# Delta rule: ScalarE's affine step on the turned output stays in its PSUM bank, VectorE's gate product reads it there, and the steps of all four engines are put in another order

## What is computed

```
q, k, v = silu(causal_conv4(x @ Wq)), silu(causal_conv4(x @ Wk)), silu(causal_conv4(x @ Wv))
alpha, beta = sigmoid(x @ Wa + ba), sigmoid(x @ Wb + bb)
for each token t:
    err = S k_t - v_t
    S = alpha_t S - beta_t err k_t^T
    o_t = S q_t
o = layernorm(o) * ln_w + ln_b            # over the 128 values of a head
o = o * sigmoid(x @ Wg)                   # the gate
y = o @ Wo
```

## Time and profile before

| what | value |
|---|---|
| runs | median 1885.67 us of 3 (1882.06 to 1886.81) |
| profiled execution | 1887.38 us, its span 1885.6 us, TensorE's mean granted clock 0.977 |
| busy in the span | PE 1781.6, PEld 1315.9, DVE 1529.9, ACT 1286.9, POOL 941.3 us |
| four laps, 812.0 to 949.4 us | 137.40 us: PE busy 135.95, DVE 125.06, ACT 105.42, POOL 86.21 us, clock 1.00 |
| the gate product (L1910), 64 times | 675 / 1152 / 2193 ns (least, median, most) |
| the affine step (L1804), 64 times | 768 / 772 / 777 ns |

### The profile page before, as it was taken

The page is one execution under the profiler, slowest core; times in us unless marked ns, Lnnn a source line. Parts: engine busy times, 40 slices in busy tenths (PEclk is TensorE's granted clock), DMA queues, the critical chain, the costliest instruction groups (busy, mean ns, idle before and its releaser), DMA issues.

```text
span 1885.6 us, 49242 instructions
## 1 busy us (share of the span) xinstructions
PE 1781.6 (94%) x19366; PEld 1315.9 (70%) x19366; DVE 1529.9 (81%) x2561; ACT 1286.9 (68%) x2850; POOL 941.3 (50%) x1890
## 2 busy tenths in 40 slices
PE   8889999999899889999999999999999999999687
PEld 4733333332688767888888888888888888887576
DVE  6699999993466567989989999899899898998455
ACT  2068888889342357778777777787777777777553
POOL 1134344445223244666566566666666566565233
PEclk9989999999899999999999999999999999999889
DMA  6201212110100111111111111111111111110101
GB/s 184 85 17 35 59 35 59 34 47 8 29 1 1 56 35 36 49 38 35 49 49 35 39 50 38 35 50 49 35 50 38 35 50 38 35 38 20 45 1 45
DMA packets 74133, 78.61 MB, mean 42 GB/s; under 512 B 13168, under 2 KB 60784, under 8 KB 73904
## 3 DMA queue, kind: packets, MB, share of 16 engines
q1 hardware_dynamic: 73904, 75.46, 13.6%
HBM read 66.13 MB, written 8.91 MB: 40 GB/s over the span
## 4 chain that ended last, share of the span: by engine, by line
PE 38%; ACT 14%; DVE 9%; issue 4%; POOL 1%; POOLq 0%; ACTq 0%; DVEq 0%
PE ps L1530 10%; PE ps L1678 5%; PE ps L1560 4%; DVE d_acc L1833 3%; PE ps L1660 3%; ACT d_kq L1717 3%; ACT d_tt L1769 2%; PE ps L1648 2%; PE ps L1654 2%; PE ps L1630 2%; ACT d_acc L1701 2%; PE ps L1637 2%; DVE d_o_g L1910 2%; PE ps L2008 1%; ACT d_ty L1766 1%
## 5 line engine op out<-in xcount | busy, mean ns | idle before, releaser
L1833 DVE SCALAR_TENSOR_TENSOR d_acc<-ps,d_par,d_acc 128x1023 f32<-128x1023 f32 (+2 forms) x288 | 366.1, 1271 | 25.7 <-ACT d_acc L1701 25.5
L601 ACT ACTIVATE a_prob<-ps 128x512 f32<-128x512 f32 (+2 forms) x640 | 309.3, 563 | 99.1 <-PE ps L567 93.9
L1530 PE MATMUL ps<-x1p,d_wh 128*128 128x512 f32 x1024 | 358.7, 431 | 7.1 <-DVE d_acc L1833 7.1
L623 DVE TENSOR_REDUCE a_mx<-ps 128x2 f32<-128x1024 f32 (+2 forms) x320 | 336.5, 1112 | 34.9 <-PE ps L551 27.2
L1530 PE MATMUL ps<-x1p,d_wl 128*128 128x512 f32 x512 | 203.1, 397 | 0.0
L510 POOL TENSOR_SCALAR_AFFINE_SELECT a_prob<-a_prob 128x128 f32<-128x128 f32 (+1 forms) x384 | 125.2, 330 | 125.1 <-ACT a_prob L601 114.1
L567 PE MATMUL ps<-q,k 51*128 51x512 bf16 (+2 forms) x640 | 175.1, 365 | 2.5 <-ACT a_prob L601 0.9
L1701 ACT ACTIVATE d_acc<-ps,d_par 128x512 f32<-128x512 f32 x192 | 145.8, 776 | 42.5 <-PE ps L1530 40.4
L1530 PEld LDWEIGHTS ps<-x1p,d_wh 128*128 128x128 f32 x1024 | 161.1, 191 | 18.4 <-DVE d_acc L1833 8.1
L1785 ACT ACTIVATE d_w_sb<-ps 128x128 f32<-128x128 f32 x256 | 70.5, 275 | 144.9 <-PE ps L1648 144.2
L581 PE MATMUL ps<-a_prob,a_v 128*32 128x512 f32 (+3 forms) x1536 | 165.0, 502 | 0.4 <-POOL a_prob L510 0.2
(11 more groups left out here) (244 smaller groups left out, 4557.4 us busy)
## 6 DMA issues: line engine op xcount, KB each, us to landing
d_abc<-scratch_alpha SPq DMA_DIRECT2D x32, 512.0 KB, 3.9
d_gb<-scratch_g SPq DMA_DIRECT2D x32, 512.0 KB, 4.0
d_wr<-in_dw SPq DMA_DIRECT2D x16, 512.0 KB, 3.5
scratch_q<-p_parts SPq DMA_DIRECT2D x24, 128.0 KB, 2.4
q<-scratch_q SPq DMA_DIRECT2D x32, 96.0 KB
scratch_y<-a_oT SPq DMA_DIRECT2D x64, 36.0 KB
x_tok<-in_x SPq DMA_DIRECT2D x4, 512.0 KB, 7.6
q<-scratch_q SPq DMA_DIRECT2D x32, 64.0 KB
```

Source lines behind the costliest of these rows:

```text
L601: inc(nc.scalar.activation(prob[:, y % PB, g:g + heads, off:], ps[:, PLACE["st", n, x], 0:heads * w].rearrange("p (h c) -> p h c", c=w), A ...
L623: inc(nc.vector.tensor_reduce(out, ps[:, bank:bank + 2, 0:heads * w].rearrange("p r (h c) -> p r h c", c=w), AX.X, ALU.max, negate=True), ...
L1530: last = nc.tensor.matmul(ps[:, bank, :], wp[g][:, k, i, :], x(part), start=(k == 0 and j == 0), stop=(k == KE - 1 and j == 2))
L1833: inc(nc.vector.scalar_tensor_tensor(acc[i][:, d:T], taps[:, 0:T - d], par[p][:, 4 * i + j:4 * i + j + 1], acc[i][:, d:T], ALU.mult, ALU.a ...
```

## The change

ScalarE writes the affine step's result back into the PSUM bank that it read, instead of into `o_g` in SBUF. VectorE's gate product reads that bank and writes `o_g`. So `o_g`'s reuse (`og_l` of unit n-2) is now waited for by VectorE and no longer by ScalarE, and the ring frees `o_turn`'s bank with the gate product (`gated`) instead of with the affine step.

```diff
         def o_turn(n, j):                                        # PE
-            bank = ring(n, ("o_turn", j), ("affine", n, j + 1))
+            bank = ring(n, ("o_turn", j), ("gated", n, j + 1))
...
             W("o_turned", n, j + 1)                              # ACT
-            W("og_l", n - 2, j + 1)
-            inc(nc.scalar.activation(o_g[n % 2][:, j * HALF:(j + 1) * HALF], ps[:, BANK[n, "o_turn", j], :], ACT.Identity, bias=ln2[:, 1:2],
+            bank = ps[:, BANK[n, "o_turn", j], :]
+            inc(nc.scalar.activation(bank, bank, ACT.Identity, bias=ln2[:, 1:2],
                                      scale=ln2[:, 0:1]), "affine")
...
             W("affine", n, j + 1)                                # DVE
+            W("og_l", n - 2, j + 1)
             c = slice(j * HALF, (j + 1) * HALF)
-            inc(nc.vector.scalar_tensor_tensor(o_g[n % 2][:, c], gate[n % 2][:, c], 1.0, o_g[n % 2][:, c], ALU.add, ALU.mult), "gated")
+            inc(nc.vector.scalar_tensor_tensor(o_g[n % 2][:, c], gate[n % 2][:, c], 1.0, ps[:, BANK[n, "o_turn", j], :], ALU.add, ALU.mult), "gated")
```

All four lists of `ORDER` are replaced. The new ones, cut to the stretches that matter below:

```diff
 "PE"
+ L.proj.0.0.0 L.proj.0.0.1 O.ks.2 ... S.k_turn.0 O.w.3 O.qs.3 O.s.3 O.pw.3 S.k_turn.1 O.ks.4 O.qs.4 X.o_turn.0 O.w.4 X.o_turn.1 O.s.4 O.pw.4
+ ... O.ks.6 S.z32 O.w.6 O.qs.6 S.v_turn.0 O.s.6 S.y64 O.ks.7 O.pw.6 S.gate.0.0 S.v_turn.1 O.w.7 S.z64 O.qs.7 O.pw.7 S.gate.0.1 L.proj.2.0.0
+ S.y128 L.proj.2.0.1 L.proj.2.1.0 L.proj.2.1.1 S.z128 L.pair.0 L.pair.1 S.w.0 L.pair.2 S.s.0 X.out.0 L.pair.3 S.ks.1 S.pw.0 X.out.1 S.qs.1
+ S.w.1 X.out.2 S.pw.1 S.s.1 X.out.3
 "ACT"
+ ... S.spread O.w.5 X.og.0 S.y32 O.pw.5 X.og.1 L.tap.1.0 O.w.6 L.tap.1.1 S.diag S.y64 S.v_turn.0 O.pw.6 O.w.7 S.v_turn.1 S.z64 L.silu.0 O.pw.7
 "DVE"
+ X.o_turn.0 S.k_turn.1 S.turned O.pw.3 O.s.5 X.o_turn.1 O.ks.6 S.whole ... S.s.1 L.lanes S.pw.0 S.ks.2 X.out.1 X.out.2 X.out.3 ... L.columns S.ks.5
 "POOL"
- S.solve.1 S.solve.2 S.solve.3 S.solve.4 S.qg X.og.0 L.scalars O.wo L.split O.stats X.og.1 L.solve.0
+ S.solve.4 O.wo X.og.0 L.split X.og.1 L.scalars O.stats S.qg L.solve.0 L.solve.1 L.solve.2 L.solve.3
```

More of the change, by code:

```diff
@@ L1244 @@
     "PE": """
[L1245 to L1248, removed]
@@ L1249 @@
-        S.qs.4 S.s.4 S.pw.4 E.proj.1.0.0 S.ks.5 E.proj.1.0.1 S.w.5""",
+        L.proj.0.0.0 L.proj.0.0.1 O.ks.2 L.proj.0.1.0 O.w.2 L.proj.0.1.1 O.qs.2 O.s.2 O.pw.2 O.gate.1.0 O.ks.3 O.gate.1.1 S.k_turn.0 O.w.3 O.qs.3
+        O.s.3 O.pw.3 S.k_turn.1 O.ks.4 O.qs.4 X.o_turn.0 O.w.4 X.o_turn.1 O.s.4 O.pw.4 L.proj.1.0.0 O.ks.5 L.proj.1.0.1 L.proj.1.1.0 O.w.5 O.qs.5
+        S.y32 O.s.5 O.pw.5 L.proj.1.1.1 O.ks.6 S.z32 O.w.6 O.qs.6 S.v_turn.0 O.s.6 S.y64 O.ks.7 O.pw.6 S.gate.0.0 S.v_turn.1 O.w.7 S.z64 O.qs.7 O.pw.7
@@ L1250 @@
+        S.gate.0.1 L.proj.2.0.0 S.y128 L.proj.2.0.1 L.proj.2.1.0 L.proj.2.1.1 S.z128 L.pair.0 L.pair.1 S.w.0 L.pair.2 S.s.0 X.out.0 L.pair.3 S.ks.1
+        S.pw.0 X.out.1 S.qs.1 S.w.1 X.out.2 S.pw.1 S.s.1 X.out.3""",
     "ACT": """
-        O.w.1 S.blocks O.pw.1 O.w.2 L.tap.0.0 S.silu.2 L.tap.0.1 O.pw.2 O.w.3 X.norm.0 O.gate.1 O.pw.3 S.v_turn.0 O.w.4 X.norm.1 O.pw.4 O.w.5
-        X.o_turn.0 L.tap.1.0 O.pw.5 S.spread L.tap.1.1 O.w.6 S.y32 X.o_turn.1 S.v_turn.1 X.og.0 O.pw.6 S.diag O.w.7 S.y64 L.silu.0 S.z64 O.pw.7
@@ L1253 @@
-        L.silu.1 S.y128 L.tap.2.0 L.tap.2.1 S.gate.0 S.z128 S.w.0 S.pw.0 X.og.1""",
+        S.tap.2.0 S.tap.2.1 O.gate.0 O.z128 O.w.0 X.norm.0 O.pw.0 O.w.1 S.blocks O.pw.1 X.norm.1 L.tap.0.0 O.w.2 L.tap.0.1 O.pw.2 O.w.3 O.gate.1
+        O.pw.3 O.w.4 S.silu.2 X.o_turn.0 X.o_turn.1 O.pw.4 S.spread O.w.5 X.og.0 S.y32 O.pw.5 X.og.1 L.tap.1.0 O.w.6 L.tap.1.1 S.diag S.y64 S.v_turn.0
+        O.pw.6 O.w.7 S.v_turn.1 S.z64 L.silu.0 O.pw.7 S.y128 L.silu.1""",
     "DVE": """
-        O.s.5 O.pw.2 S.columns O.pw.3 O.ks.6 O.pw.4 S.turned X.o_turn.0 L.conv.1.0 O.s.6 S.whole O.ks.7 L.conv.1.1 O.pw.5 O.pw.6 L.conv.1.2 S.k_turn.0
@@ L1256 @@
-        S.k_turn.1 X.o_turn.1 O.pw.7 L.decay O.stats L.conv.2.0 L.pair.0 L.conv.2.1 S.s.0 L.pair.1 L.pair.2 S.ks.1 L.conv.2.2 L.pair.3 S.s.1 X.out.0
-        S.ks.2 S.pw.0 L.lanes S.s.2 X.out.1 S.ks.3 E.conv.0.0 S.s.3 E.conv.0.1 S.ks.4 E.conv.0.2 S.pw.1 S.s.4 X.out.2 S.ks.5 X.out.3""",
+        X.o_turn.0 S.k_turn.1 S.turned O.pw.3 O.s.5 X.o_turn.1 O.ks.6 S.whole O.pw.4 O.pw.5 O.s.6 L.conv.1.0 O.ks.7 L.conv.1.1 L.conv.1.2 O.pw.6
+        O.pw.7 O.stats L.decay L.conv.2.0 L.pair.0 L.pair.1 L.pair.2 S.s.0 L.conv.2.1 S.ks.1 X.out.0 L.pair.3 L.conv.2.2 S.s.1 L.lanes S.pw.0 S.ks.2
@@ L1258 @@
+        X.out.1 X.out.2 X.out.3 S.s.2 E.conv.0.0 S.ks.3 E.conv.0.1 S.pw.1 S.s.3 L.k_turn.0 S.ks.4 E.conv.0.2 S.pw.2 S.s.4 L.columns S.ks.5""",
     "POOL": """
-        S.solve.1 S.solve.2 S.solve.3 S.solve.4 S.qg X.og.0 L.scalars O.wo L.split O.stats X.og.1 L.solve.0""",
+        S.solve.4 O.wo X.og.0 L.split X.og.1 L.scalars O.stats S.qg L.solve.0 L.solve.1 L.solve.2 L.solve.3""",
 }
```

## The result

The changed kernel takes 1909.15 us, the median of 4 runs (1904.36 to 1910.38), against 1886.09 (1882.06 to 1886.81): a ratio of 1.0121 with a 95% interval from 1.0103 to 1.0138. It is slower by 23 us, where 11 were forecast; the direction and the range held, the size did not.

The account below looks back on a forecast made before the run. TensorE was taken to bound the kernel: work 33.5 and waits 1.5, taken as 34.9 us a lap against 34.39. 31 x 0.5 = +15.5, end -4, on 1887.4 gives 1898.9; median 1.7 lower: 1897 us, range 1868 to 1912.

Parts of the forecast that it names:

- The edit's price: VectorE's gate product reading PSUM was to take 0.68 us instead of 1.15 median; ScalarE's affine step was left at 0.77.
- The rival of the failed edit: Reading and writing one bank slows ScalarE or VectorE, 0.5 to 1 us a lap more: 1912 to 1928; chance 0.05.
- VectorE's relief becomes idle time: What VectorE saves shows as 1 to 2 us idle ahead of `columns` each lap, not in the lap.
- The faster rival: VectorE's saving carries through because the waits fall away: lap 34.0, near 1870 us; chance 0.28.
- The second loop: Loop through GpSimd, `lanes` to `columns` and back to `y64`'s copy: T+34.8, no later than the 34.9 lap.
- `s.3` and `s.4`: TensorE steps waiting for ScalarE's copy of w in the new order: 0.41 and 0.19 us a lap.
- `z64` waits for `y64`: TensorE's `z64` waits for ScalarE's copy `y64`, which stands behind `diag`: 4.40 against TensorE's 3.78, wait 0.62 us.
- `pair.1` "still waits ... now about 0.3, since `pair.0` stands later": TensorE's `pair.1` waits for ScalarE's tanh of the gate: 0.48 us before, about 0.3 in the new order.
- The waits, "1.5": TensorE's waits per lap in the new order, for `s.3`, `s.4`, `z64` and `pair.1`: 1.5 us together.
- the uncovered price: Time from w to s where nothing covers ScalarE's copy: 0.85 us, perhaps 0.1 too high in three places.
- The work, "33.5": Sum of TensorE's step prices over the new list of a lap: 33.5 us, against 33.1 for the old list.
- The end: After the laps, GpSimd's `og.1` stands ahead of `O.stats`, so the last block's norm starts sooner: -4 us, between 0 and -5.

Follow-up runs that it names:

- the run with `k_turn.1`: The changed kernel with TensorE's `S.k_turn.1` moved from behind `O.pw.3` to between `O.qs.3` and `O.s.3`: 1908.48 us, ratio 1.0117.
- three kernels in which one wait went: Changed kernel with one move each: TensorE's `k_turn.1` ahead of `s.3`, 1908.48 us; VectorE's `k_turn.1` and `o_turn.0` ahead of `columns`, 1909.70; ScalarE's second `v_turn` copy behind `z128`, 1911.60.

## Why the forecast was right in direction and short in size

- **The edit's price: right.** 0.68 was taken for the gate product and 678 ns is the median. The affine step into PSUM, left at 0.77 between wide bounds, takes 748 ns instead of the 772 before. The rival of the failed edit is out, by these rows and by the edit on the old order. Also the rule that was weighed: the 65 ns more of a PSUM source aren't there, 678 ns against a least of 675 with both operands in SBUF.
- **VectorE's relief becomes idle time: right.** 1.5 us a lap ahead of `columns` (1 to 2 forecast). The faster rival rested on the relief carrying through; in the lap shown the chain it counted on has left VectorE altogether.
- **The second loop ends no earlier: right**, with slack. That it would decide from 0.1 us more was too near; filling its idle time moved nothing.
- **`s.3` and `s.4`:** 0.41 and 0.19 forecast, 0.6 together; 0.7 measured, and that only since each of the two takes 0.1 longer itself. That this wait can't be covered singly was not foreseen: it is the recurrence's own length, and the run with `k_turn.1` showed it.
- **`z64` waits for `y64`: right**, 0.62 forecast, 0.61 measured.
- **`pair.1` "still waits ... now about 0.3, since `pair.0` stands later": wrong.** It waits 0.56 in the lap shown, 0.7 by the weight load's longest, and takes 0.97 instead of 0.87 behind that. The prediction counted the old wait down by a shift of `pair.0`, and did not add up ScalarE's list from `y64` to the tanh: two turns of v, `z64`'s three copies, `y128`'s two, three copies behind `pw` and `w`, `silu` twice and two taps, all in one unbroken run. `pair.0` stands later by 0.76, but the tanh by 1.0. The lap lost little by this, and that was luck: the work from `z64` to `pair.0` was put 0.21 too high (6.39, and 6.18 from 857.24 to 863.42), so `pair.1` starts 7.61 behind `z64` where the sum had 7.56.
- **The waits, "1.5": the step that failed; 2.5 measured.** 0.7 for `s.3` and `s.4`, 0.6 for `z64`, 0.66 for `pair.1`, and 0.6 for short steps that the sum priced at 0.22. In this lap `s.5`, `w.6`, `ks.7` and `qs.7`, all behind small blocks, and `w.5`, which waits for its residual, take 0.32 or 0.33 each, and `ks.4` 0.27. For that there was no term. It could have been read before: behind the step of small blocks that starts at 849.57 stands `pw` at 850.23, and the trace has the next start at 850.55, 0.32 on. The prediction leaned the other way: it took 34.9 instead of its sum of 35.0, because the uncovered price "may be 0.1 too high".
- **The work, "33.5": 0.7 too high.** 35.28 - 2.5 leaves 32.8. A triplet that stands behind another triplet takes 0.68 to 0.69 (861.35 to 862.03), where the row that was taken gave 0.81 (855.19 to 856.00); that triplet stood right behind a step of small blocks, and had the same 0.1 on it. Three of the six steps of small blocks take 0.61 or 0.62, not 0.66. The sum itself is 0.1 high too: the prediction's own prices over its own list give 33.4.
- **Sum:** 31 x 0.5 = +15.5 was forecast for the laps, +27.6 came. The two errors go against each other: waits 1.0 too low, work 0.7 too high, and the lap was then taken 0.1 under the sum. 1.0 - 0.7 + 0.1 = 0.4, and the lap is 35.28 rather than 34.9: 12 us. By place, the stretch from `w.6` to `pair.1`, where ScalarE decides, was put at 11.96 and took 12.04 (852.81 to 864.85); the rest of the lap was put at 23.04 and took 23.24. So the stretch on ScalarE came out nearly as summed, and of the 0.4 only 0.1 lies there. The end gave -5.0 where -4 was counted, and the first laps -1.7 where 0 was. That makes 20.9 between the profiled executions; the medians lie 2 us further apart than these.

What stays open: the prices of the chains that end close to each other in the lap of after (ScalarE's run, the recurrence, `w.0`'s copy) were not isolated in kernels of their own; that they are near each other is argued from three kernels in which one wait went and the lap stayed within 0.15. Nor is it isolated which part of the new order makes the laps longer: that the order does is shown, that it does so by these waits is read from the traces. No version that was tried is clearly faster than the kernel before; the edit on the old order comes nearest, with ratios of 0.9982 and 0.9994.

## What to carry to other kernels

When a list of steps is rearranged, take the price of a step from rows with the same neighbours: a step behind a wait or behind small blocks costs 0.1 us more here, and eight of these in a lap are 0.8 us. Add up each engine's list between the two points where it meets the bounding engine, on ScalarE as on TensorE; scaling an old wait by a shift misses what was put ahead of it. Look too at what else hangs on the order, such as which bank a step is given. A wait that goes and leaves the time as it was is not refuted as a cost: look for the wait that came up in its place (here `ks.4` for the state, `w.0` for v), and move work into the latency instead of around it. And judge an edit and a new order apart: here the edit was free, the order cost 2.3%, and together they looked like an edit that costs 1.2%.

## What the runs showed of the hardware

- A VectorE product of 128x512 with both operands in SBUF takes 0.68 us alone; when it meets a GpSimd instruction it ends 0.54 to 0.56 us behind the end of that (46 meetings in the run of the order alone, the two shown 1.20 and 1.28 long). With one operand in PSUM it takes 0.68 beside the same instruction. Median 1152 against 678 ns over 64 of them.
- ScalarE's affine step of 128x512 is 24 ns shorter with its output in PSUM: 748 against 772 ns; in the other pair of kernels, the edit on the old order and the order alone, 745 and 773. The Trainium skill (ScalarE: Activation LUTs, the section Step-by-step: what each stage is for) says that writing to PSUM is faster than to SBUF, without a size; the rows agree.
- A 128x128 step of TensorE that had to wait, or that follows a step of small blocks, took 0.32 to 0.33 us to the next start instead of 0.22 in the lap shown (0.27 behind a very short wait). The next projection triplet starts 0.68 to 0.69 behind a triplet that itself follows another one or `out`, 0.78 behind one that follows a short step (858.36 to 859.14), and 0.81 behind one that follows small blocks.
- The recurrence of one chunk, from one w to the next over ScalarE's copy, s, state, ks and residual, takes 2.72 us where only `qs` and `pw` stand between.
